# 1/sqrt by Ln and Exp with one table, and another order of steps in attention's last two groups: a three-stage kernel on one core

## The reference

```
x = x + 0.5 * ffn(LN(x));  x = x + attn(LN(x));  x = x + 0.5 * ffn(LN(x))
ffn(x):  gamma = softmax(x @ w_router.T + b_router); the 2 largest of 8 experts
         y = sum over the two of (x @ w_expert.T + b_expert)        # 256 -> 256
attn(t): q, k, v = split(t @ w_qkv); 16 heads of 16; causal softmax(q k / 4) v
         x = proj(out) + b_proj + t
         (x - mean(x)) * rsqrt(var(x) + 1e-5) * ln_gamma + ln_beta
```

## Time and profile before

| | |
|---|---|
| runs | 1023.23 us median of 3 (1022.47 to 1023.43) |
| the profiled execution | 1024.88 us, span 1023.2 us |
| PE busy | 966.8 us, 94% |
| DVE busy | 838.1 us, 82% |
| ACT busy | 513.6 us, 50% |
| POOL busy | 261.8 us, 26% |
| mean granted clock of PE | 0.975 of full |

### The profile page before, as it was taken

One profiled execution on the slowest core, in us unless ns is written; L12 is line 12 of the kernel. 1 busy time (PEld: TensorE's weight loads), 2 busy tenths in 40 slices (PEclk: granted clock), 3 DMA queues, 4 the chain that ended last, 5 costly groups with the idle time before them and its releaser, 6 DMA issues.

```text
span 1023.2 us, 18097 instructions
## 1 busy us (share of the span) xinstructions
PE 966.8 (94%) x5602; PEld 575.6 (56%) x5602; DVE 838.1 (82%) x2476; ACT 513.6 (50%) x1027; POOL 261.8 (26%) x289
## 2 busy tenths in 40 slices
PE   6899999999888699999999999999887999999997
PEld 5678887888655233333333333333343777777776
DVE  6677776777675899999999999999756888888775
ACT  4225433442322277777777777777776333232210
POOL 1012212221420421221222222222333443434211
PEclk9999999999996599999999999999998999999999
DMA  6201101112113412222222323322320112110001
GB/s 220 86 1 62 63 0 62 62 46 78 62 49 78 123 29 69 72 70 71 71 72 75 76 76 75 76 75 75 85 64 8 47 62 63 62 53 20 10 21 41
DMA packets 55059, 64.27 MB, mean 63 GB/s; under 512 B 13777, under 2 KB 37313, under 8 KB 54977
## 3 DMA queue, kind: packets, MB, share of 16 engines
q1 hardware_dynamic: 54384, 62.47, 21.4%
q10 hardware_dynamic: 592, 0.80, 0.2%
HBM read 41.30 MB, written 21.23 MB: 61 GB/s over the span
## 4 chain that ended last, share of the span: by engine, by line
PE 83%; DVE 7%; ACT 3%; issue 3%; DMA 2%; SPq 1%; POOL 1%; DVEq 0%; POOLq 0%; ACTq 0%
PE bank L353 39%; PE bank L1312 13%; PE bank L1485 13%; PE bank L1469 12%; PE bank L345 2%; PE bank L792 2%; DMA c_rec<-att_rec 1%; ACT b_probs L1448 1%; DMA v_all<-L_ffn_w_experts 1%; DVE bank L1339 1%; DVE c_acc L989 1%; PE bank L743 1%; DVE b_neg L1343 1%; DVE a_acc L989 1%; DVE a_st L308 1%
## 5 line engine op out<-in xcount | busy, mean ns | idle before, releaser
L1448 ACT ACTIVATE b_probs<-bank 128x512 f32<-128x512 f32 (+1 forms) x608 | 302.4, 587 | 108.5 <-PE bank L1469 108.3
L1312 PE MATMUL bank<-b_ks,b_qs 96*128 96x512 bf16 (+3 forms) x768 | 226.8, 338 | 18.4 <-DVE b_neg L1339 6.2
L1339 DVE CUSTOM_DVE_ANT_0 bank<-bank,b_below 128x384 f32<-128x384 f32 (+3 forms) x512 | 234.9, 516 | 2.4 <-PE bank L1312 0.8
L1469 PE MATMUL bank<-b_qs,b_ks 99*128 99x512 bf16 (+3 forms) x768 | 215.3, 331 | 4.7 <-ACT b_probs L1448 4.6
L353 PE MATMUL bank<-we,a_xt 128*128 128x512 f32 x768 | 190.7, 402 | 2.0 <-DVE a_acc L989 2.0
L353 PE MATMUL bank<-we,c_xt 128*128 128x512 f32 x768 | 187.7, 399 | 1.1 <-DVE c_acc L989 1.1
L1422 POOL TENSOR_SCALAR_AFFINE_SELECT b_probs<-b_probs 128x512 f32<-128x512 f32 x128 | 81.5, 642 | 339.1 <-ACT b_probs L1448 339.1
L1343 DVE TENSOR_REDUCE b_neg<-bank 128x1 f32<-128x512 f32 x256 | 160.6, 679 | 3.6 <-PE bank L1312 2.1
L353 PEld LDWEIGHTS bank<-we,a_xt 128*128 128x128 f32 x768 | 143.2, 191 | 30.8 <-DVE a_acc L989 1.7
L353 PEld LDWEIGHTS bank<-we,c_xt 128*128 128x128 f32 x768 | 141.9, 189 | 32.5 <-DVE c_acc L989 1.6
L1485 PE MATMUL bank<-b_probs,b_vs 128*32 128x512 f32 (+3 forms) x1536 | 154.5, 496 | 0.9 <-POOL b_probs L1422 0.9
(11 more groups left out here) (135 smaller groups left out, 887.8 us busy)
## 6 DMA issues: line engine op xcount, KB each, us to landing
b_qs<-q_parts SPq DMA_DIRECT2D x96, 128.0 KB, 3.0
b_ks<-k_parts SPq DMA_DIRECT2D x96, 128.0 KB, 3.1
q_parts<-a_part SPq DMA_DIRECT2D x16, 384.0 KB, 2.7
k_parts<-a_part SPq DMA_DIRECT2D x16, 384.0 KB, 2.7
att_num<-b_oev SPq DMA_DIRECT2D x64, 64.0 KB, 2.2
c_num<-att_num SPq DMA_DIRECT2D x8, 512.0 KB
c_rec<-att_rec SPq DMA_DIRECT2D x16, 256.0 KB
out<-xs SPq DMA_DIRECT2D x8, 512.0 KB, 3.1
```

The costliest lines, as they stand in the source:

```text
L1312: last = nc.tensor.matmul(ms[bank][:, a * width:(a + 1) * width], qs[g.u][0:ROWS, c, i * P:(i + 1) * P], ks[g.u][0:ROWS, c, lo:lo + width] ...
L1339: last = dve.tensor_tensor_reduce(part, part, below[:, CH - width:CH], -1.0, 3.0e38, ALU.add, ALU.min, dst[:, a, :])
L1448: act.activation(probs[b % 4][:, heads[0]:heads[0] + hp, 0:width], es[exp_bank(g, unit)][:, 0:hp * width].rearrange("p (h w) -> p h w", w= ...
L1469: last = nc.tensor.matmul(es[exp_bank(g, unit)][:, a * width:(a + 1) * width], ks[g.u][:, c, j * P:(j + 1) * P], qs[g.u][:, c, first_q:fir ...
```

## The change

The square root and the reciprocal become Ln and Exp of -0.5 times its result, both on ACT. A table set is named at the start of ACT's program, ahead of its weight loads. Since ACT now writes `ln`, it first waits until the tiles that use its last values are made (xh_ready, y_ready). In group 14, DVE's two `attended` go from ahead of the turn of the maxima to behind it. In group 15, ACT's roots of both norms go from behind block 6 to behind block 4, PE's second projection from block 3 to 2, PE's turn from 6 to 7, the router with the logits from 8 to 9, the turn of the logits from 9 to 10. In all groups POOL's copy of the values goes from block 4 to 2.

```diff
--- before.py
+++ after.py
@@ -313,17 +313,17 @@
             last = dve.bn_aggr(mv_[:, t, :], st_[:, t, :])
         last.then_inc(n_ag, 1)
 
-    def norm_scale(dve, m, mv_, std_, out_ln, n_sd, n_rc, n_rd):
-
-        dve.wait_ge(n_sd, at(m + 1))
-        dve.reciprocal(out_ln[:, :, 0:1], std_[:]).then_inc(n_rc, 1)
+    def norm_scale(dve, m, mv_, out_ln, n_rc, n_rd):
+
         dve.wait_ge(n_rc, at(m + 1))
         dve.scalar_tensor_tensor(out=out_ln[:, :, 1:2], in0=mv_[:, :, 0:1], scalar=-1.0, in1=out_ln[:, :, 0:1],
                                  op0=ALU.mult, op1=ALU.mult).then_inc(n_rd, 1)
 
-    def std_of(act, m, mv_, std_, n_ag, n_sd):
+    def inverse_std(act, m, mv_, log_, out_ln, n_ag, n_lg, n_rc):
         act.wait_ge(n_ag, at(m + 1))
-        act.activation(std_[:], mv_[:, :, 1:2], ACT.Sqrt, bias=s.eps[:, 0:1]).then_inc(n_sd, 1)
+        act.activation(log_[:], mv_[:, :, 1:2], ACT.Ln, bias=s.eps[:, 0:1]).then_inc(n_lg, 1)
+        act.wait_ge(n_lg, at(m + 1))
+        act.activation(out_ln[:, :, 0:1], log_[:], ACT.Exp, scale=-0.5).then_inc(n_rc, 1)
 
     def normalize(act, dst, src, ln_, done):
         for t in range(TPC):
@@ -573,7 +573,8 @@
             act.activation(ybias[pair][:].rearrange("p t d -> p (t d)"), pb[:], ACT.Copy).then_inc(q.bias_ready, 1)
 
         def spread(m):
-            std_of(act, m, mv, std, q.normed_aggr, q.std_done)
+            act.wait_ge(q.xh_ready, at(m))
+            inverse_std(act, m, mv, std, ln, q.normed_aggr, q.std_done, q.rstd_done)
 
         def norm(m):
             act.wait_ge(q.norm_ready, at(m + 1))
@@ -583,7 +584,7 @@
 
 
         def norm2(m):
-            std_of(act, m, mv2, std2, q.aggr2, q.std2)
+            inverse_std(act, m, mv2, std2, s.ln2[:, tiles(m), :], q.aggr2, q.std2, q.rstd2)
             act.wait_ge(q.norm2, at(m + 1))
             act.wait_ge(q.turned2, at(m))
             act.sem_inc(q.apart, 1)
@@ -620,8 +621,12 @@
             act.sem_inc(q.apart, 1)
             normalize(act, resid, xs_tile(m), ln2_of(m), q.resid_ready)
 
+        def spread3(m):
+            act.wait_ge(q.y_ready, at(m))
+            inverse_std(act, m, mv3, std3, ln3, q.aggr3, q.std3, q.rstd3)
+
         def norm3(m):
-            std_of(act, m, mv3, std3, q.aggr3, q.std3)
+            spread3(m)
             act.wait_ge(q.norm3, at(m + 1))
             act.wait_ge(q.scaled, at(m))
             normalize(act, yn, lambda t: xa[:, t, :], lambda t, n: ln3[:, t, n:n + 1], q.y_ready)
@@ -657,13 +662,14 @@
                     qk_mid(c - 1, j + 1)
 
         if first:
+            nc.scalar.preload_act_table_set("natural_log_exp_and_others")
             act.dma_start(wr_in[:], s.w_router).then_inc(q.router_in, 16)
             act.dma_start(be_in[:], s.b_experts).then_inc(q.bias_in, 16)
             act.dma_start(s.brouter[:], s.b_router).then_inc(q.router_in, 16)
             act.dma_start(wqk_in, s.w_qk).then_inc(q.qk_in, 16)
             act.dma_start(wv_in, s.w_v).then_inc(q.v_in, 16)
             act.wait_ge(q.consts, 3)
-            act.activation(unused[:], s.eps[:, 0:1], ACT.Sqrt)
+            act.activation(unused[:], s.eps[:, 0:1], ACT.Exp)
             weights_hi((0,))
             spread(0)
             norm(0)
@@ -688,13 +694,13 @@
                 if (early, block) == (0, 2):
                     residual(1)
                 if (early, block) == (0, 1):
-                    std_of(act, 0, mv3, std3, q.aggr3, q.std3)
-                if (early, block) == (0, 6):
-                    std_of(act, 0, mv, std, q.normed_aggr, q.std_done)
-                    std_of(act, 1, mv3, std3, q.aggr3, q.std3)
+                    spread3(0)
+                if (early, block) == (0, 4):
+                    spread(0)
+                    spread3(1)
                 if (early, block) == (0, 7):
                     split_hi(0, 0)
-                if (early, block) == (0, 8):
+                if (early, block) == (0, 9):
                     logits_out(0)
 
             a.scalar(act, lead)
@@ -870,14 +876,14 @@
                     project(0, 0, (0,))
                 if (early, block) == (1, 11):
                     project(0, 0, (1,))
-                if (early, block) == (0, 3):
+                if (early, block) == (0, 2):
                     project(1, 1, (0,))
                     project(1, 1, (1,))
-                if (early, block) == (0, 6):
+                if (early, block) == (0, 7):
                     turn(0)
-                if (early, block) == (0, 8):
+                if (early, block) == (0, 9):
                     router(0, 0)
-                if (early, block) == (0, 9):
+                if (early, block) == (0, 10):
                     turn_logits(0)
 
             a.tensor(pe, lead)
@@ -924,13 +930,13 @@
             norm_stats(dve, xs_tile(m), m, st, mv, q.normed_stats, q.normed_aggr)
 
         def scale(m):
-            norm_scale(dve, m, mv, std, ln, q.std_done, q.rstd_done, q.norm_ready)
+            norm_scale(dve, m, mv, ln, q.rstd_done, q.norm_ready)
 
         def norm2(m):
             dve.wait_ge(q.x_ready, at(TPC * m + TPC))
             dve.sem_inc(q.apart, 1)
             norm_stats(dve, xs_tile(m), m, st2, mv2, q.st2, q.aggr2)
-            norm_scale(dve, m, mv2, std2, s.ln2[:, tiles(m), :], q.std2, q.rstd2, q.norm2)
+            norm_scale(dve, m, mv2, s.ln2[:, tiles(m), :], q.rstd2, q.norm2)
 
         def split_lo(m, par):
             for h in range(DK):
@@ -1014,7 +1020,7 @@
             norm_stats(dve, lambda t: xa[:, t, :], m, st3, mv3, q.st3, q.aggr3)
 
         def scale3(m):
-            norm_scale(dve, m, mv3, std3, ln3, q.std3, q.rstd3, q.norm3)
+            norm_scale(dve, m, mv3, ln3, q.rstd3, q.norm3)
 
         def slot(c, par, nth):
             if first and exists(c - 1):
@@ -1086,7 +1092,7 @@
                 dve.tensor_tensor(s.xs[:, tiles(m), :], yg[:], xb[:], ALU.add).then_inc(q.x2_ready, 1)
 
             def lead(early, block):
-                if (early, block) == (1, 23):
+                if (early, block) == (1, 24):
                     dve.wait_ge(a.v_copied, at(NG))
                     attended(0, 0, 0)
                     attended(1, 1, 0)
@@ -1421,7 +1427,7 @@
 
                     pool.affine_select(out=part, in_=part, compare_op=ALU.is_ge, fill=0.0, base=0,
                                        pattern=[[0, GH], [1, P]], channel_multiplier=-1).then_inc(kept, 1)
-                if b == 4 and exists(g + 1):
+                if b == 2 and exists(g + 1):
                     pool.wait_ge(summed, at(nkb * g.n))
                     copy_values(pool, g + 1)
                 lead_step(lead, g, b)
```

## The result

Median of the changed kernel 1024.67 us (17 runs, 1021.42 to 1025.88) against 1022.70 us (17 runs, 1021.95 to 1024.14) for the kernel before on the same chip: ratio 1.0018, 95% interval 1.001 to 1.0025. Forecast were 1021.1 us and 1018.9 to 1023.4. Measured a second time on another chip (e11_changed_again) it had 1024.10 against 1023.48, ratio 1.0008 (0.9999 to 1.0017). So it is 0.1 to 0.2% slower, though the second interval just takes in no change, where I had forecast 0.2% faster. The profiled execution of the changed kernel took 1024.39 us, with a span of 1022.7.

A forecast was written before the change was run, and what follows sets the result against it. PE was taken as the bound, busy 94% of the span, with gains only where it idles, 745 to 790 us. Terms +0.4 - 0.3 - 2.1 = -2.0 us gave 1022.9 profiled, 1021.1 as median; range 1018.9 to 1023.4.

The forecast's parts named there:

- the hand-over in group 15: End of the last group: last copy at about 787.5, third stage at 787.6 instead of 789.76, -2.1 us over both groups.
- the signs of being wrong: Stall after block 4 under 2 or above 6 us, PE waiting for the mask at the hand-over, ACT's pair above 0.8.
- rival B: Gain drowns: norms cost +0.8, later turn and router hold the mask, third stage only 1.0 earlier; 1022.7 us, chance 0.20.
- C, the aggregates late on DVE: ACT's wait at block 4: chunk 1's aggregates still come at 769.15, ACT goes on 3.4 us later; 1024.5 us, chance 0.12.
- The stall at block 4: Last group: ACT waits 3 to 4 us for c_mv; PE's gap moves here, some 4.2 us, with the lower clock afterwards.
- -0.4 for group 15: Last group of attention: all its moves together bring the third stage 0.4 us earlier, beyond the 1.7 from the group before.
- Group 14, -1.7: Last group but one: b_turned copied right behind PE's turn, so the last group starts at 749.9 instead of 751.62, -1.7 us.
- Norms, +0.4: Every normalization: Ln and Exp cost 0 to 0.24 us more; five on PE's chain at 0.08 each, +0.4 us.
- Loads, -0.3: First exponential of attention: the table load at 349.88 goes, giving back 0.2 to 0.4 us, taken as -0.3.
- One load left: Start of the kernel: of seven table loads of 1.28 us only the first stays, ahead of ACT's weight DMAs, costing nothing.
- the values' copy at nothing: Each of 15 groups: POOL's 0.61 us copy at block 2 instead of 4 delays block 3's selection but costs nothing.

The follow-up runs named there:

- e11_changed_again: The changed kernel itself with no edit, measured again on another chip: 1024.10 us, ratio 1.0008 to the kernel before.
- e3: The changed kernel with POOL's add of the residual waiting until the mask is made: 1022.20 us, ratio 0.9989.
- e9: The changed kernel with ACT's norms back at block 6 and POOL's residual add waiting for the mask: 1016.62 us, ratio 0.9933.
- e10: The order of before with Ln, Exp and one table, but router and logits_out at block 9, turn of the logits at 10: 1022.95 us, ratio 0.9985.
- e7: The changed kernel with ACT's norms back at block 6, all else of the new order kept: 1018.89 us, ratio 0.9946.
- e12: The order of before with Ln, Exp and one table, but second projection at block 2 and turn of c_xh at 7: 1017.64 us, ratio 0.9939.
- e1: The changed kernel with all of the order of before, so only Ln, Exp and the one table are left: 1019.99 us, ratio 0.9963.
- e2: The kernel before with the new order alone, square roots and seven table loads kept: 1027.45 us, ratio 1.0044.
- e4: The changed kernel with chunk 1's inverse root on ACT at block 5 instead of 4: 1021.16 us, ratio 0.9987.
- e6: The order of before with Ln, Exp and one table, but the two attended products behind the turn of the maxima: 1019.87 us, ratio 0.9957.
- e5: The changed kernel with POOL's residual add waiting for the mask and chunk 1's inverse root at block 5: 1021.0 us, ratio 0.9967.
- e8: The order of before with Ln, Exp and one table, but ACT's norms at block 4 instead of 6: 1020.42 us, ratio 0.9958.

## Why the prediction was wrong

**The step that failed** is the hand-over in group 15: "The last copy ends at about 787.5; the third stage starts at 787.6 instead of 789.76". Counted from the group's start, the forecast was 34.7 us to the last unit (784.6 less 749.9), measured 34.29 (782.33 less 748.04); 37.1 to the mask, measured 36.31. Until there the hand count was right within 0.8. From there it gave the mask the 0.40 us that it had before and PE's projection 3.69. I had moved the logits by a block and looked at what stood around them on PE and ACT, not at what POOL does beside DVE at 784: the residual's add of 2.34 us, which before came 1.42 us after the mask's start. That made turn_mask wait 1.87 us; the projection started 38.97 us into the group instead of 37.7, and took 2.57 longer. Together 3.84 us, which is the whole of leg C's excess: 45.20 measured, 41.4 forecast (41.81 less 0.4). That PE waits for the mask at the hand-over was one of the signs of being wrong that the prediction named. e3, e9 and e10 show the cause from both sides. In the six profiles in which PE waits for the mask the projection takes 5.35 to 6.32 us, in seven of the eight others 3.69. How far it cools varies: 6.26 in the changed kernel, 5.36 in e7, and 5.38 in e12 with no wait for the mask.

**The sign of the hand-over** was rival B's: the mask holds the gain. B priced it at 1.1 us, by lateness alone, and came to 1022.7. C, the aggregates late on DVE, did not occur.

**The stall at block 4** came as forecast: ACT 3.50 us, PE 4.51 (forecast 4.2) at the lower clock afterwards. What was wrong was not to ask what the same order would be without it. I booked the gap as moved, from the turn to block 5, and so as free; but the turn at block 7, with the projection at block 2, had removed the gap at the turn already (e12 has these two moves alone, and no wait there). e7 against the changed kernel puts the price at 5.60 us of leg C and 0.72% of the ratio on other chips (0.62% against e11). Of the 5.60, 3.59 are idle time of PE (4.51 less 0.92) and 0.90 the colder projection (6.26 less 5.36); the rest was not taken apart. The single sum of -0.4 for group 15 hid four terms, which the kernels part one by one in leg C: the loads of the last group -2.61 (41.81 before, 39.20 in e1), the new order without its two faults -2.58 (36.62 in e9), the mask beside the add +2.98 (39.60 in e7), the stall at block 4 +5.60 (45.20). The last two depend on which is priced first: the stall alone costs 6.51 (43.13 in e3 less 36.62), and then the mask only 2.07. In e3 the granted clock behind the same gap was 0.50 from 764.57 to 773.57, in the changed kernel from 765.04 to 768.04 only.

**Group 14, -1.7.** b_turned at 733.17 and the projection without a wait are as forecast, the size is not: leg B is 0.53 shorter. In e2 to e4, at full clock, it is 13.75, which is 1.95 shorter, but so it is in e1 with the old order, where the c_rec loads came early. In the changed kernel PE's clock fell behind the turn of the maxima (0.54 from 734 to 736; the product at 735.12 takes 3.12 us), which puts 1.4 us back.

**Norms, +0.4.** 0.03 us for a pair, so by that one row 0.15 for the five on the chain. **Loads, -0.3.** Too small, but by how much is open. In leg A the two kernels with the load have 386.85 and 386.39, the twelve without it 384.34 to 385.87, in the mean 1.46 us less. Much of that is the clock: in seven profiles (before, e2; e1, e3, e4, e6, e12) it was still 0.50 from 4 to 6 us behind the first scores, in the other seven 0.81 or more. Among those seven the kernels without the load have 385.79 to 385.87, so 0.5 to 1.1 us less. I had counted only PE's idle time of 0.42 at 351.83; why more comes back is not shown. **One load left, and the values' copy at nothing:** both right, the turn of the maxima comes every 26.24 us in both kernels.

**In sum:** the median is 3.6 us above the forecast. The profiled execution is 1.5 above its own (1024.39, forecast 1022.9): leg C is 3.8 longer than forecast, while A and B together are 3.0 shorter than before (402.55 to 399.54), forecast 2.0, and what lies ahead of the first scores and behind the experts' first product gave 0.9 more, where 0.4 was to be lost. The other 2.1 come from going over to the median: I took off the 1.65 by which the profile before lay above its runs and some 0.1 in rounding, and the changed kernel's lies 0.28 below its own. That rows of one execution say what a median does is only argued.

**What stays open:** when PE's clock falls behind a short wait. At the turn of the maxima, with 1.57 us of idle time in each kernel, it fell in seven profiles (the changed kernel twice, e5, e7 to e10) and not in the other seven. They are the same seven in which it rose early behind attention's first scores: there leg A is 384.34 to 385.10, in the others of the changed norms 385.79 to 385.87. So what such a profile loses in B it had gained in A, wholly or in part: A and B together are 399.54 in the changed kernel and 400.28 in e5, where the clock fell, and 399.54 and 399.55 in e3 and e4, where it held. No run tests what ties the two moments together.

## What to carry to other kernels

Before an operation of DVE is moved, look at what POOL does at the new time: an operation of 0.2 us waited for the whole of a 2.3 us add, and the hand-over behind it went cold. Put the short one that another engine waits for ahead of the long one that nobody does. Where two edits are aimed at one wait, price each on the kernel that already has the other: here the later turn with the earlier projection was a gain (e12), the earlier norm alone nothing (e8), and both together a loss (leg C of e3 against e1).

## What the runs showed that I had not expected

A DVE operation that takes 0.21 us alone takes 0.40 beside POOL's selection (before) and 2.39 beside its add, while DVE's four statistics take 1.39 us at 786.66, beside POOL's next add, and 1.41 at 794.03, with POOL idle. The table load doesn't hold up the DMAs that ACT issues: load from 0.82 to 2.10, first issue at 0.85, the fifth at 2.60, where the kernel before had 0.82 and 2.60 without a load beside them. ACT's wait for its own result costs 0.03 us (Ln ends at 24.63, Exp starts at 24.66). And the start of attention varies by 3.9 us between executions of the same code, more than the whole effect under study, and the granted clock there differs: from 240 to 300 us it was 1.00 in e1 and e4, which start attention at 345.5, and 0.94 and 0.97 in e11 and e8, which start it at 348.2 and 349.4. That nothing else adds to it was not shown.
